# A four-layer graph attention kernel: rows between the layers kept unscaled, their roots taken once a layer

## The chip, the cores and the metric

The kernel runs on one core of a Trainium2 chip. The metric is device microseconds (us) of one execution, as a median over runs; lower is better. Engines are called PE (TensorE), DVE (VectorE), ACT (ScalarE), POOL (GpSimd) and SP (the queue that issues most DMAs).

## The reference, cut to what matters

```python
# N = 50000 nodes, E = 12500 edges sorted by target, D = 128
h = relu(layernorm(x)); x = x + conv(h)            # a graph convolution
h = relu(layernorm(x))
for l in range(4):                                 # _gat_layer
    h = x_l @ W[l]; e = ea @ We[l]
    alpha = leaky_relu((h @ a_s)[src] + (h @ a_d)[dst] + e @ a_e, 0.2)
    alpha = segment_softmax(alpha, dst)            # over the edges into one node, and a self loop
    out = segment_sum(h[src] * alpha, dst) + b
    x_l = (out - mean(out)) * rsqrt(var(out) + 1e-5) * g + beta
out = x + x_4
```

Every node has a self loop. A node without an incoming edge needs only its own row: that is the dense part. Nodes with edges, at most 12500 of them, go through the graph part.

## The kernel before, in words

Edges lie in 100 tiles (`C`) of 125 (`P`). `S` holds for each edge the row of its source node, `T` the row of its target node; one extra tile of `T` (index `C`) holds rows of segments that cross a border between tiles. A row has 130 numbers (`W`): the 128 features and two scores, which come out of the same matrix product, since the attention vectors are two more columns of the weights (`WCX`). The mean is taken out through centred weights, so the variance is the mean of the squares.

After setup and the convolution, the kernel runs four times:

1. **Dense stage** (`dense`, 16 groups of 500 nodes): all nodes through everything, with dense arithmetic. Beside it POOL issues 100 indirect gathers (`refresh`, L1535) that fetch into `S` the rows of the last layer from the DRAM table `row_t`.
2. **Score stage** (first block of `attention`, L1547 to L1615): the score columns are turned by PE transposes, then one long chain on DVE over arrays of 100x125 does the softmax. ACT takes the exponents; SP loads the masks `M` meanwhile.
3. **Loop** (second block of `attention`): 50 pairs of tiles. For pair n: DVE `mask` (L1779) and POOL `diagonal` (L1663) make the weights, PE `aggregate` (L1689, L1691) sums edges into target rows, ACT `copy_t` (L1739) copies them out of PSUM, PE `multiply_t` (L1710) multiplies by the weights, DVE `add_bias_t` (L1805) adds the bias into `T`. The source rows get the same product: PE `turn` (L200), DVE `copy_s` (L1801), PE `multiply_s` (L1710), DVE `add_bias_s` (L1811). Then ACT `squares` (L1749, L1754) and `root` (L1761), DVE `invert` (L1817), `rescale_t` (L1834) and `rescale_s` (L1841) normalise both. DVE `edge` (L1792) keeps two columns for the crossing rows. In layers 0 to 2 SP stores `T` to `row_t` in ten chunks (L1652). Layer 3 (`final`) has no source rows; POOL scatters the result to the output instead (L216).
4. **Crossing rows**: a short serial chain over one 100-row tile, L1722 to L1728 on PE, L1768 and L1771 on ACT, L1858 and L1866 on DVE, then a store (L1654).

The order on each engine is written by hand: `run_slot(t, NU, [(lag, op), ...])` issues in slot t the operation `op` for pair t - lag, in the order of the list. Engines meet through semaphores alone. Buffers and PSUM banks rotate over four pairs (`NS`); the T product and the aggregate of a pair share a bank, as do the turned S tile and the S product. A pair is in a slot of its own on every engine, and the slot's length in a steady run is the interval at which pairs complete.

All blocks end with a barrier over the engines.

## Time and profile before

| | |
|---|---|
| median of 3 runs | 2232.75 us (2230.29 to 2233.54) |
| profiled execution | 2236.65 us, of which the span is 2234.9 us |
| granted TensorE clock, mean over the span | 0.867 |
| busy in the span | PE 74%, weight loads 55%, DVE 78%, ACT 67%, POOL 52% |
| DMA | 145.21 MB, mean 65 GB/s |

Of the span, 1371 us are the four rounds of dense stage, score stage and loop; the rest is setup, the convolution and a longer dense stage. The busy shares are means over stages with different limits, so they don't say what limits a loop. In a timeline the start-to-start distance of two instructions of one engine tells what an instruction costs its engine; the duration shown also has its last part, which overlaps the next instruction. One fp32 matrix product stands in the trace as two MATMUL records.

### The profile page before, as it was taken

The numbers are of one execution on the slowest core, as the hardware profiler recorded it, in microseconds if no ns is written. First come the engines' busy times: TensorE is split into PE (matmuls) and PEld (weight loads), VectorE is DVE, ScalarE is ACT, GpSimd is POOL, SyncE is SP. The second block draws the span as 40 slices with busy tenths as digits, with TensorE's granted clock in tenths as the row PEclk, the third lists the DMA queues.
The fourth block names the chain that finished last, engine by engine and source line by source line (L and its number), as shares of the span: only waits on it lengthen the run. The fifth ranks groups of instructions, "written<-read, shape, count | busy, mean of one in ns | idle before, by whom it ended". The sixth has DMA issues, their size and how long they took to land. (4 is left out here: it accounts for less than half of the span.)

```text
span 2234.9 us, 41269 instructions
## 1 busy us (share of the span) xinstructions
PE 1663.9 (74%) x9595; PEld 1239.8 (55%) x9595; DVE 1751.1 (78%) x8774; ACT 1496.0 (67%) x7686; POOL 1154.6 (52%) x1069
## 2 busy tenths in 40 slices
PE   2589388888488885884996884996884996984980
PEld 1589255555277773552884552884552884542760
DVE  3680599999489995895996895996995996895870
ACT  0352299999389994992765992765992765992540
POOL 0477777400045555774225774225774225773777
PEclk9995599999689996996996996996996996995985
DMA  8013323321312123113113113113113113124321
GB/s 144 21 39 97 94 66 98 87 59 43 84 36 66 53 69 78 43 47 84 37 58 88 43 47 84 36 60 86 43 47 84 36 60 87 43 47 107 90 75 35
DMA packets 123138, 145.21 MB, mean 65 GB/s; under 512 B 56197, under 2 KB 83637, under 8 KB 122145
## 3 DMA queue, kind: packets, MB, share of 16 engines
q1 hardware_dynamic: 66303, 116.40, 19.1%
q0 software_dynamic: 56160, 25.40, 5.7%
q8 instruction: 78, 1.28, 0.3%
q14 instruction: 165, 1.35, 0.2%
q10 hardware_dynamic: 432, 0.79, 0.1%
HBM read 94.60 MB, written 67.86 MB: 73 GB/s over the span
## 5 line engine op out<-in xcount | busy, mean ns | idle before, releaser
L212 POOL DMA_INDIRECT S<-row_t,rowI x400 | 540.3, 1351 | 224.0 <-issue 224.0
L944 PE MATMUL bank<-AC,XT 128*125 128x390 f32 x800 | 330.5, 519 | 0.3
L1008 ACT ACTIVATE R<-bank 125x128 f32<-125x128 f32 x1200 | 323.2, 308 | 0.0
L1008 ACT ACTIVATION_READ_ACCUMULATOR R<-bank 125x1 f32 x1200 | 278.5, 242 | 0.0
L1663 POOL TENSOR_TENSOR R<-ident,aselfS 125x250 f32<-125x250 f32 x150 | 95.3, 637 | 333.7 <-PE bank L1691 257.8
L200 PEld LDWEIGHTS bank<-ident,Y 125*128 125x128 f32 x800 | 98.4, 150 | 215.3 <-issue 150.3
L200 PE MATMUL bank<-ident,Y 125*128 125x125 f32 x800 | 131.3, 290 | 115.2 <-ACT XT L992 52.0
L1710 PE MATMUL bank<-WCX,XT 128*125 128x130 f32 (+1 forms) x1400 | 210.2, 289 | 2.6 <-ACT XT L1739 2.4
L1739 ACT ACTIVATE XT<-bank 128x250 f32<-128x250 f32 x200 | 76.0, 380 | 190.6 <-PE bank L1691 182.4
L1689 PE MATMUL bank<-R,S 125*128 125x125 f32 x800 | 174.3, 300 | 33.9 <-DVE R L1779 27.6
L1050 DVE BATCH_NORM_STATS2 st<-R 125x6 f32<-125x128 f32 x800 | 173.0, 278 | 31.5 <-issue 31.1
L1710 PEld LDWEIGHTS bank<-WCX,XT 128*125 128x125 f32 x1400 | 184.1, 190 | 11.9 <-ACT XT L1739 4.9
L212 POOL DMA_INDIRECT S<-in_x,srcI x100 | 131.3, 1313 | 112.0 <-issue 112.0
L924 PEld LDWEIGHTS bank<-AC,XT 128*125 128x125 f32 x800 | 105.8, 204 | 117.4 <-ACT SB L1025 109.5
L924 PE MATMUL bank<-AC,XT 128*125 128x128 f32 x800 | 125.1, 303 | 58.5 <-ACT SB L1025 54.0
L216 POOL DMA_INDIRECT out_rows<-T,repNI x101 | 122.7, 1215 | 74.6 <-DVE T L1831 44.3
L944 PEld LDWEIGHTS bank<-AC,XT 128*125 128x125 f32 x800 | 134.4, 197 | 45.2 <-issue 10.4
L1689 PEld LDWEIGHTS bank<-R,S 125*128 125x128 f32 x800 | 124.6, 196 | 62.0 <-DVE R L1779 51.7
L1691 PE MATMUL bank<-R,T 125*128 125x125 f32 x800 | 158.8, 281 | 0.0
L212 POOL DMA_INDIRECT T<-in_x,dstI x101 | 136.1, 1348 | 40.6 <-issue 40.6
L1030 ACT ACTIVATE R<-bank 125x128 f32<-125x128 f32 x400 | 107.9, 313 | 39.9 <-PE bank L928 38.4
L207 PE MATMUL bank<-W,R 128*125 128x128 f32 x800 | 129.7, 311 | 0.0
(425 smaller groups left out, 5122.1 us busy)
## 6 DMA issues: line engine op xcount, KB each, us to landing
row_t<-T SPq DMA_DIRECT2D x40, 568.8 KB
R<-in_x SPq DMA_DIRECT2D x100, 224.0 KB
out_rows<-R SPq DMA_DIRECT2D x100, 224.0 KB
R<-m_t SPq DMA_DIRECT2D x5, 2734.4 KB
S<-row_t,rowI POOLq DMA_INDIRECT x400
T<-in_edge_attr SPq DMA_DIRECT2D x1, 5600.0 KB
x_t<-XB SPq DMA_DIRECT2D x50, 112.0 KB
R<-x_t SPq DMA_DIRECT2D x25, 224.0 KB
```

What stands on the lines that cost most here:

```text
L200: ins = nc.tensor.transpose(ps[:, a * P:(a + 1) * P], t, ident[0:P, 0:P])
L207: ins = nc.tensor.matmul(pz[0:P, a, :], xt[:, a * P:(a + 1) * P], w, start=False, stop=True, skip_group_check=True)
L212: pool.indirect_dma_start(to, None, table, bass.IndirectOffsetOnAxis(ap=idx, axis=0), bounds_check=rows - 1, oob_is_err=False).then_inc(do ...
L216: pool.indirect_dma_start(table, bass.IndirectOffsetOnAxis(ap=idx, axis=0), frm, None, bounds_check=rows - 1, oob_is_err=False).then_inc(d ...
L924: nc.tensor.matmul(last_of(g)[:, a, :], h0(g, a), AC[3], start=a == 0, stop=False, skip_group_check=True)
L944: nc.tensor.matmul(LAYERS[a][0:P, 0:3 * D + 6], h0(g, a), ACB[:, 0:3 * D + 6], start=True, stop=True).then_inc(layers_done.s, 1)
L1008: ins = nc.scalar.activation(JUNK[:, a * 3 + l, :], LAYERS[a][0:P, l * D:(l + 1) * D], ACT.Square, scale=D ** -0.5, accum_out=NRM[:, g % N ...
L1030: ins = nc.scalar.activation(JUNK[:, 12 + a, :], last_of(g)[:, a, :], ACT.Square, scale=D ** -0.5, accum_out=ss4[:, g % NS, a:a + 1])
L1050: ins = nc.vector.bn_stats(ring[:, a, :], v[:, a, :])
L1689: nc.tensor.matmul(o, S[:, 2 * n + a, 0:D], MA[:, r, a, :], start=True, stop=False, skip_group_check=True)
L1691: ins = nc.tensor.matmul(o, T[:, 2 * n + a, 0:D], DGB[:, r, a, :], start=False, stop=True, skip_group_check=True)
L1710: ins = nc.tensor.matmul(product(banks[bank + r], 2 * P)[:, a, :], XT[:, r, xt + a * P:xt + (a + 1) * P], WCX[:, l, 0:cols], start=not fin ...
```

## The change

Rows between layers 0, 1, 2 and 3 are kept unscaled. A row has 131 numbers (`RW`): the new column holds the mean of squares, which ACT's `squares` writes straight into it. `row_t` has rows of 131 numbers. In layers 0 to 2 `root`, `invert`, `rescale_t` and `rescale_s` are gone from the loop. At the head of the score stage of layers 1 to 3 ACT takes the roots of the whole column at once, DVE inverts them and scales the score columns before PE turns them; the inverse is multiplied into the edge weights (`alphaS`, `aselfS`, `DG`) and, for the source rows, into `add_bias_s`, which becomes two instructions for a pair instead of one. The order of every loop engine is rewritten: of layers 0 to 2 on PE, ACT and DVE, of the final layer on ACT. The crossing rows are copied unscaled, and their square stands in the same column.

```diff
+RW = W + 1
-        S = sb("S", [P, C, W])
-        T = sb("T", [P, TC, W])
+        S = sb("S", [P, C, RW])
+        T = sb("T", [P, TC, RW])
-        row_t = nc.dram_tensor("row_t", [P * TC, W], F32, kind="Internal").ap()
+        row_t = nc.dram_tensor("row_t", [P * TC, RW], F32, kind="Internal").ap()
...
+                    if l:
+                        dve.wait_ge(*rooted.at(1))
+                        ch.add(nc.vector.reciprocal(sx[:, 1:2], sx[:, 0:1]))
+                        ch.link(nc.vector.reciprocal(rrT[:, :], rrT[:, :]))
+                        nc.vector.tensor_scalar(sx[:, 3:5], T[0:C, C, D:W], sx[:, 1:2], None, ALU.mult)
+                        nc.vector.tensor_tensor(scT[:, :, :], T[:, 0:C, D:W],
+                                                rrT[:, :].unsqueeze(2).broadcast_to([P, C, 2]),
+                                                ALU.mult).then_inc(scored.s, 1)
+                        dve.wait_ge(*rooted.at(2))
+                        ch.link(nc.vector.reciprocal(rrS[:, :], rrS[:, :]))
+                        nc.vector.tensor_tensor(scS[:, :], S[:, :, D], rrS[:, :], ALU.mult).then_inc(scored.s, 1)
                     dve.wait_ge(*columns_in.at(1))
...
+                    if l:
+                        nc.vector.tensor_tensor(alphaS[:, :], banks[0][0:P, 0:C], rrS[:, :], ALU.mult)
+                        nc.vector.tensor_tensor(aselfS[:, :], banks[0][0:P, C:2 * C], rrT[:, :], ALU.mult)
+                        nc.vector.tensor_scalar(DG[:, :], ident[0:C, 0:C], car1[:, 1:2], sx[:, 1:2], ALU.mult, ALU.mult)
...
+                    if l:
+                        nc.scalar.activation(rrT[:, :], T[:, 0:C, W], ACT.Sqrt, bias=epsc[:, 0:1])
+                        nc.scalar.activation(sx[:, 0:1], T[0:C, C, W:RW], ACT.Sqrt,
+                                             bias=epsc[0:C, 0:1]).then_inc(rooted.s, 1)
+                        nc.scalar.activation(rrS[:, :], S[:, :, W], ACT.Sqrt, bias=epsc[:, 0:1]).then_inc(rooted.s, 1)
                     act.wait_ge(*act_in.at(1))
...
-                        run_slot(t, NU, [(0, aggregate), (1, multiply_t)] if final else [(4, multiply_s), (4, multiply_t), (3, aggregate), (0, turn)])
+                        run_slot(t, NU, [(0, aggregate), (1, multiply_t)] if final else [(3, multiply_t), (0, turn), (2, multiply_s), (1, aggregate)])
...
+                            ins = nc.scalar.activation(Y[:, r, a, :], T[:, 2 * n + a, 0:D], ACT.Square, scale=D ** -0.5,
+                                                       accum_out=T[:, 2 * n + a, W:RW])
+                        ins.then_inc(t_ready.s, 1)
...
-                        run_slot(t, NU, [(4, squares), (2, copy_t), (4, root)])
+                        run_slot(t, NU, [(3, root), (1, copy_t), (2, squares)] if final else [(2, squares), (0, copy_t)])
...
-                        nc.vector.tensor_tensor(S[:, 2 * n:2 * n + 2, :], product(banks[4 + n % NS], 2 * P),
-                                                BB[:, l:l + 1, :].broadcast_to([P, 2, W]), ALU.add).then_inc(bias_s.s, 1)
+                        for a in range(2):
+                            z = product(banks[4 + n % NS], 2 * P)[:, a, :]
+                            if l:
+                                ins = nc.vector.scalar_tensor_tensor(S[:, 2 * n + a, 0:W], z, rrS[:, 2 * n + a:2 * n + a + 1],
+                                                                     BB[:, l, :], ALU.mult, ALU.add)
+                            else:
+                                ins = nc.vector.tensor_tensor(S[:, 2 * n + a, 0:W], z, BB[:, l, :], ALU.add)
...
-                        run_slot(t, NU, [(0, diagonal), (0, mask), (4, rescale_t), (3, invert), (1, edge)] if final else [(0, mask), (1, add_bias_s), (0, copy_s), (1, add_bias_t), (2, edge), (3, invert), (5, rescale_t), (3, rescale_s)])
+                        run_slot(t, NU, [(0, diagonal), (0, mask), (4, rescale_t), (3, invert), (1, edge)] if final else [(0, mask), (2, add_bias_t), (1, add_bias_s), (0, copy_s), (4, edge)])
...
+                    if not final:
+                        dve.wait_ge(*x_pe.at(3))
+                        stage(nc.vector.tensor_copy(T[0:C, C, 0:W], banks[2][0:C, 0:W]), 3)
+                        return
```

The order of DVE in one slot of the loop of layer 1, before; `bank4` to `bank7` hold products of source rows, `bank0` to `bank3` those of target rows, `rr4` is the inverse root:

```order
L1779 TENSOR_TENSOR R<-R,alphaS 125x250
L1811 TENSOR_TENSOR S<-bank4,BB 125x260
L1801 COPY XT<-bank5 128x250
L1805 TENSOR_TENSOR T<-bank0,BB 125x260
L1792 COPY EDGE<-XT 128x4
L1817 RECIPROCAL rr4<-rt4 125x4
L1834 TENSOR_TENSOR T<-T,rr4 125x260
L1841 TENSOR_TENSOR S<-S,rr4 125x260
```

And in the changed kernel, with lines of its own file:

```order
L1824 TENSOR_TENSOR R<-R,alphaS 125x250
L1850 TENSOR_TENSOR T<-bank1,BB 125x2x130
L1859 SCALAR_TENSOR_TENSOR S<-bank6,rrS,BB 125x130 x2
L1846 COPY XT<-bank7 128x250
L1837 COPY EDGE<-XT 128x4
```

Three instructions of a slot are gone, one became two, and the T bias now stands ahead of the S bias and belongs to the pair before it.

PE in one slot of the same loop, before:

```order
L1710 MATMUL bank5<-WCX,XT 125x130 x2
L1710 MATMUL bank1<-WCX,XT 125x130 x2
L1689 MATMUL bank2<-R,S 128x125
L1691 MATMUL bank2<-R,T 128x125
L1689 MATMUL bank2<-R,S 128x125
L1691 MATMUL bank2<-R,T 128x125
L200 MATMUL bank5<-ident,S 128x125 x2
```

And changed (L1748 is the product, L205 the transposes, L1727 and L1729 the aggregate):

```order
L1748 MATMUL bank1<-WCX,XT 125x130 x2
L205 MATMUL bank4<-ident,S 128x125 x2
L1748 MATMUL bank6<-WCX,XT 125x130 x2
L1727 MATMUL bank3<-R,S 128x125
L1729 MATMUL bank3<-R,T 128x125
L1727 MATMUL bank3<-R,S 128x125
L1729 MATMUL bank3<-R,T 128x125
```

The ten products and transposes are the same; the two products now stand apart with the transposes between them, and the T product runs one aggregate later than the S product.

DVE at the head of the score stage of layer 1 in the changed kernel; before, the stage begins with the multiplication of `bank2`:

```order
L1568 RECIPROCAL sx<-sx 100x1
L1569 RECIPROCAL rrT<-rrT 125x100
L1570 TENSOR_SCALAR sx<-T,sx 100x2
L1571 TENSOR_TENSOR scT<-T,rrT 125x200
L1575 RECIPROCAL rrS<-rrS 125x100
L1576 TENSOR_TENSOR scS<-S,rrS 125x100
L1564 TENSOR_TENSOR tmp<-bank2,repN 100x125
```

Six instructions stand ahead of what was the first one, and PE's three transposes wait for them.

## Rows read from the trace of the kernel before

**Rows 1.** Stages: dense, loop of layer 1, final loop; busy us per engine, PE clock.
```profile
1192.50:1370.00 177.50, 134.27 (x576) 79.53 (x576) 142.04 (x832) 139.69 (x800) 134.91 (x100) 0.85 0.24 57
...
1391.00:1527.00 136.00, 119.89 (x908) 109.79 (x906) 126.49 (x404) 88.61 (x504) 31.34 (x50) 0.96 0.16 49
...
2060.40:2235.00 174.60, 105.27 (x658) 87.40 (x658) 92.14 (x355) 60.47 (x304) 122.73 (x101) 0.77 0.28 71
```

**Rows 2.** Groups by form, layer 0's loop: count, busy us, mean ns, idle before.
```profile
L1841 DVE TENSOR_TENSOR S<-S,rr 125x260 f32<-125x260 f32 x42 | 33.3, 793 | 0.0
...
L1663 POOL TENSOR_TENSOR R<-ident,aselfS 125x250 f32<-125x250 f32 x39 | 24.9, 637 | 74.4 <-PE bank L1691 74.4
...
L1834 DVE TENSOR_TENSOR T<-T,rr 125x260 f32<-125x260 f32 x42 | 16.4, 391 | 0.0
```

**Rows 3.** Timeline, a steady slot of layer 0: start us, duration us.
```profile
1110.32 0.41 DVE L1779 TENSOR_TENSOR R<-R,alphaS 125x250 f32<-125x250 bf16 x1
...
1112.02 0.64 POOL L1663 TENSOR_TENSOR R<-ident,aselfS 125x250 f32<-125x250 f32 x1 [1.91 <-PE bank L1691]
1112.12 0.82 DVE L1841 TENSOR_TENSOR S<-S,rr 125x260 f32<-125x260 f32 x1
...
1112.87 0.41 DVE L1779 TENSOR_TENSOR R<-R,alphaS 125x250 f32<-125x250 bf16 x1
...
1113.20 0.41 DVE L1811 TENSOR_TENSOR S<-bank,BB 125x260 f32<-125x260 f32 x1
...
1113.33 0.49 PE L1689 MATMUL bank<-R,S 125*128 125x125 f32 x2 [0.21 <-DVE R L1779]
```

**Rows 4.** Timeline, first slots of layer 1's loop.
```profile
1396.53 1.13 PE L1710 MATMUL bank<-WCX,XT 128*125 128x130 f32 x8
...
1397.24 0.43 DVE L1811 TENSOR_TENSOR S<-bank,BB 125x260 f32<-125x260 f32 x1 [0.67 <-PE bank L1710]
...
1398.60 1.13 PE L1710 MATMUL bank<-WCX,XT 128*125 128x130 f32 x8
...
1399.56 0.38 PE L1689 MATMUL bank<-R,S 125*128 125x125 f32 x2
...
1403.74 0.60 POOL L1663 TENSOR_TENSOR R<-ident,aselfS 125x250 f32<-125x250 f32 x1 [2.44 <-PE bank L1691]
1403.77 0.84 DVE L1779 TENSOR_TENSOR R<-R,alphaS 125x250 f32<-125x250 bf16 x1
```

**Rows 5.** Timeline, two DVE instructions on PSUM, final loop.
```profile
2074.62 0.60 DVE L1824 SCALAR_TENSOR_TENSOR T<-bank,rr,G 125x128 f32<-125x128 f32 x2
```

**Rows 6.** Timeline, end of layer 1's loop and its crossing rows.
```profile
1516.15 0.39 PE L1691 MATMUL bank<-R,T 125*128 125x125 f32 x2
...
1521.82 0.43 PE L1722 MATMUL bank<-ident,EDGE 128*100 128x128 f32 x1 [4.10 <-DVE T L1834]
...
1525.69 0.29 ACT L1771 ACTIVATE sx<-sx,epsc 100x1 f32<-100x1 f32 x1
...
1526.66 0.28 SPq L1654 DMA_DIRECT2D row_t<-T  x1
```

**Rows 7.** Timeline, score stage of layer 1.
```profile
1370.68 0.43 PE L1596 MATMUL bank<-ident,S 125*100 125x125 f32 x1 [8.34 <-PEq L872]
...
1371.57 0.29 DVE L1555 TENSOR_TENSOR tmp<-bank,repN 100x125 f32<-100x125 f32 x1 [3.72 <-PE bank L1598]
...
1386.98 0.94 DVE L1583 RECIPROCAL mx<-mx 100x125 f32<-100x125 f32 x1
```

**Rows 8.** Stages again, inside that score stage (last numbers: DMA share, GB/s).
```profile
1384.00:1386.00 2.00, 0.13 (x1) 0.13 (x2) 1.64 (x6) 0.00 (x0) 0.00 (x0) 0.50 0.00 0
```

**Rows 9.** Timeline, head of the final loop.
```profile
2068.44 1.28 ACT L1761 ACT_TABLE_LOAD   x1
...
2072.92 1.23 POOL L216 DMA_INDIRECT out_rows<-T,repNI  x1 [38.98 <-DVE T L1831]
```

**Rows 10.** Timeline, first ACT instruction of the dense stage of layer 1.
```profile
1198.15 0.30 ACT L974 ACTIVATE rt<-mv,epsc 125x4 f32<-125x4 f32 x1 [6.76 <-DVE mv L1057]
```

133 lines of the change are left out of this document (69 added, 64 removed).

## The prediction, made before the changed kernel was timed

> **What bounds the kernel now.** I read the table of stages first [rows 1]. Layer 1's round is a dense stage of 177.5 us, a score stage of some 21 us and a loop with its crossing rows of 136 us; layers 0 and 2 are like it. The change leaves the dense arithmetic alone, so three loops of 136 us are where time can come from. In a loop DVE is busy for 126.5 us of the 136, PE for 119.9, ACT for 88.6, POOL for 31. Busy times overlap, so next comes the timeline of one steady slot [rows 3]: `mask` starts at 1110.32 and again at 1112.87, 2.55 us later, and between them DVE has no gap. PE, on the other hand, starts its aggregate only after a wait for that `mask`. So DVE sets the pace.
>
> One of its instructions stands out: `rescale_s` takes 793 ns in the mean, `rescale_t` of the same shape 391 [rows 2]. POOL's `diagonal` runs from 1112.02 to 1112.66 [rows 3]; `rescale_s` starts at 1112.12 and ends at 1112.94, just 0.28 us behind POOL's end. At 1403.77 it is `mask` that starts 0.03 us behind POOL and then takes 0.84 us instead of 0.41 [rows 4]. So a DVE instruction with both inputs in SBUF that begins while POOL's works is held until POOL is done. The Trainium skill says the same (SBUF — State Buffer, section Who interferes with whom): the second input of such an instruction comes through a read interface that GpSimd also uses, whoever starts first keeps it, and an instruction with at most one SBUF input is not touched. By that rule, with which the trace agrees in those two rows, the hold isn't removed with `rescale_s`; it looks for `mask`, the only such instruction left in the slot. That is my first rival.
>
> What is next below DVE? In the first slots of layer 1's loop, before `rescale_s` is in play, PE's products start at 1396.53 and 1398.60 [rows 4]: 2.07 us a slot, with no idle time of PE noted. That is PE's own pace for its ten products and transposes at the full clock.
>
> **The loop of layers 0 to 2.** DVE, start to start: 2.55 us, less 0.75 for `rescale_s` (1112.12 to 1112.87, the hold in it), less 0.31 for `rescale_t` (0.391 less the 0.08 by which instructions overlap, as in `mask`, 0.41 long and 0.33 to the next one [rows 3]), leaves 1.49; `invert` goes too, worth under 0.1, left in as reserve. `add_bias_s` cost 0.33 and becomes two. Two such instructions on PSUM, 128 columns each, take 0.60 us [rows 5], so 0.52 to the next: plus 0.19, 1.68 in all. In layer 0 the two are plain additions, between 0.33 and 0.52; DVE has then 1.5 to 1.7. The Trainium skill (VectorE: DVE Perf Modes, section The TRN2 errata) gives a fixed 120 cycles of 0.96 GHz to each instruction that reads PSUM; by that estimate the split would cost 0.125 and not 0.19. A held `mask` adds 0.43: 2.1 us.
> ACT: 88.6 us for 50 pairs is at most 1.77 us a slot [rows 1], and `root` goes. POOL: one `diagonal` of 0.64. PE: the same ten, 2.07. So PE becomes the bound, with DVE close by. Are PE's inputs there in time? With the lags of the lists, and DVE working in the same time as PE's next slot, `aggregate` and `multiply_s` take what DVE made a slot before, `multiply_t` what ACT made two slots before. The tightest round is: `multiply_s` starts, 0.71 us later DVE can start on its result (1396.53 to 1397.24) [rows 4], then 0.52 for the two bias instructions, 0.33 for `copy_s`, and the next `multiply_s` about 0.1 later: 1.66, under 2.07. For `mask` it is 0.71 + 0.52 + 0.33 + 0.07 + 0.41, some 2.04 from the start of `multiply_s`; the aggregate that needs it starts a slot and one product after that, 2.07 + 0.45. Half a microsecond of slack without the hold, none with it. I take 2.07 for layer 0 and 2.10 for layers 1 and 2.
> Some five slots at the head already run at PE's pace, and PE starts at the half clock there in both kernels. So 45 slots count: 45 x 0.48 = 21.6 us in layer 0, 45 x 0.45 = 20.2 in layers 1 and 2.
>
> **The end of the loop.** Before, the last aggregate stands at 1516.15 and the first crossing product at 1521.82, 5.67 us later, after a wait for `rescale_t` [rows 6]. Lags of four and five slots become two and three; `root`, `invert` and `rescale_t` are off the way. Left: copy 0.4, product 0.7, bias 0.4, squares of a pair and a half at under 1.77 a pair, some 1.8. That is 3.3: a gain of 2.3, between 0.5 and 3. In the crossing rows the root (0.29 at 1525.69) and its inverse leave the way to the store at 1526.66, and the square now waits for a copy instead of PSUM: a gain of 0.4. Together 2.7 a layer.
> Loops: 24.3 + 22.9 + 22.9 = 70.1 us.
>
> **The score stage of layers 1 to 3** now starts later. Before, PE's first transpose is at 1370.68 and DVE's first instruction at 1371.57 [rows 7]. Now: two roots on ACT, 0.29 each and overlapping, 0.5; the inverse of 100 columns, for which the row of 125 columns has 0.94, so 0.78 by columns; two scalings, 0.35; the second inverse 0.78; one scaling 0.2; then the last transpose as before. That is 2.6, less 0.1 since the two T transposes no longer stand ahead: 2.5 us. Nothing hides it: DVE's chain is serial, and the load of the masks, which SP waits for in this stage, is long over by 1384, where DMA moves nothing [rows 8], so it isn't what ends the stage either. Bounds: 2.0, if inverses overlap more, and 3.5, if each link costs another 0.2. Times three: 7.5 us lost.
>
> **Head and tail of others.** The final loop ends with POOL's scatters: 101 from 2072.92 to the end, 1.6 us apiece [rows 1, 9]. It gains what its first one gains. That waits for a root, ahead of which stands a table load of 1.28 us at 2068.44, and ACT's copy stood between squares and root; now the root follows the squares directly. Gain 1.0, between 0 and 1.5. In layers 0 to 2 the table load leaves the loop for the dense stage's first root, before which ACT idles 6.76 us [rows 10]: nothing. Rows of 131 numbers instead of 130: 0.8% more bytes in a gather, and POOL is busy 134.9 of 177.5 us there [rows 1]; nothing, at worst 1 us a stage. The memsets at the start lie beside the first loads.
>
> **Sum**: 70.1 - 7.5 + 1.0 = 63.6 us off 2236.65 of the profiled execution, which is 2173. The median shown is 3.9 lower than that execution, which would make 2169. I say 2171. With slots of 2.07 to 2.15 and the bounds above, its own range is 2163 to 2181.
>
> **Rivals.**
> A. The hold moves to `mask` and PE waits for it in every slot. For it: the row at 1403.77. POOL starts when an aggregate has ended, as it did beside `rescale_s`; from its start to the end of the held `mask` it is 0.87 us [rows 4], and I take 0.35 between PE's last aggregate record and POOL's start, since the 0.71 above is three records at 0.12 and such a rest; 0.05 comes behind the mask. PE's other work between two aggregates is its products, 0.96 (1398.60 to 1399.56) [rows 4], and of the remaining 1.11 some 0.2 for transposes, the aggregate's 0.9 apart; so the hold exceeds it by 0.1, and an aggregate after a wait starts slower by another 0.1. Slot 2.25. Against it: once PE is late, `mask`, released by another product, comes ahead of POOL and isn't held, so it should dither. Price: 45 x (0.18 + 0.15 + 0.15) = 21.6, time 2193.
> B. PE, now almost without gaps, is granted less clock. The loop has 0.96 and the dense stage 0.85 [rows 1]; at the latter a slot would be 2.07 x 0.96 / 0.85 = 2.34, loops gain 135 x 0.21 + 8.1, so 36.5, and the time is 2201. Against it: the low means hold the restarts after barriers.
> C. Slower: the new order makes PE and DVE wait for each other in turn. If the mask of a slot were needed by the aggregate of the same slot, the round would be `multiply_s` to held mask, 0.71 + 0.52 + 0.33 + 0.07 + 0.75 + 0.05 = 2.43, and the aggregate's 0.9: 3.3 us, and the time 2171 + 135 x 1.2 = 2333. It decides from a slot of 2.56 us on, since 8.1 and 1.0 gained and 7.5 lost nearly cancel. Against it: the lags put a slot between producer and consumer.
> D. The loops gain nothing, since something else than DVE paces them at 2.5. Then 2231. Against it: the 2.07 of [rows 4].
>
> **Chances.** My forecast 0.70, A 0.17, B 0.06, C 0.03, D 0.02, others on the slow side 0.02. A measurement of this kernel can tell about 0.2%, 4.5 us. Forecast, A and B are all faster: faster 0.94, within 0.2% 0.02, slower 0.04. The range takes in A: 2160 to 2193.
>
> **What would show it.** Right: in the three loops aggregates start every 2.07 to 2.15 us, PE has no idle time noted, DVE idles before its biases, waiting for products; loop stages of 112 to 114 us; score stages of layers 1 to 3 longer by 2.5 with two reciprocals of some 0.8 at the head; POOL's first scatter 11 to 12 us after the loop's start. `mask` at 0.41 in the mean speaks for me, at 0.8 with PE waiting for it for A; a clock under 0.95 in the loop for B. I am wrong if a loop stage is above 120 us.

## The result, and the profile after

| | before | changed |
|---|---|---|
| median of four runs, us | 2232.85 (2230.29 to 2233.54) | 2156.47 (2152.42 to 2159.09) |
| ratio, 95% interval | 1 | 0.9658 [0.9639, 0.9678] |
| profiled execution, span, us | 2234.9 | 2157.3 |

The change takes 76.4 us off, 3.4%. I had forecast 2171, with a range down to 2160: right in direction and in what bounds the loops before and after, too small in size. The time is 3.5 us below the range, and the largest single miss, the dense stages, is of a mechanism that the forecast left out.

The same stages as in [rows 1], of the changed kernel: the dense stage, the loop of layer 1 and the final loop. The columns are those of the rows before: stretch, its length, busy us of PE, PEld, DVE, ACT, POOL, the granted clock, DMA share, GB/s.
```profile
1165.00:1340.00 175.00, 131.80 (x576) 77.87 (x576) 142.88 (x834) 141.70 (x805) 134.33 (x100) 0.86 0.24 59
...
1361.00:1475.00 114.00, 108.35 (x908) 105.01 (x908) 94.63 (x305) 80.43 (x452) 34.03 (x50) 0.96 0.19 60
1984.00:2157.00 173.00, 100.09 (x658) 83.97 (x658) 92.05 (x356) 64.64 (x304) 122.31 (x101) 0.79 0.28 72
```
DVE's busy time in the loop fell from 126.5 to 94.6 us. PE is now busy for 108 of the loop's 111.5 us: it is the bound, as forecast. In layers 1 and 2 a hold of `mask` adds to it, as shown below.

Where the time went, by stage, in the two profiled executions. A loop is counted from its first `mask` to the store of the crossing rows; a dense stage from the start of its first statistics to the start of its last sum; "to scores" is from there to the first operation on the scores. All lengths are taken between starts in the traces, before rounding.

| us | before | changed | gain | forecast |
|---|---|---|---|---|
| first to last `mask`, layers 0, 1, 2 | 124.4, 124.3, 124.2 | 98.9, 103.6, 103.6 | 66.9 | 62.0 |
| last `mask` to store, layers 0 to 2 | 11.7, 11.7, 11.7 | 8.0, 8.0, 8.0 | 11.3 | 8.1 |
| dense, layers 1 to 3 | 170.3, 170.0, 171.0 | 167.8, 167.6, 167.6 | 8.4 | 0 |
| to scores, layers 1 to 3 | 4.4, 4.4, 4.4 | 7.2, 7.4, 9.2 | -10.6 | -7.5 |
| final loop to the end | 174.1 | 172.6 | 1.5 | 1.0 |
| sum | | | 77.5 | 63.6 |

The spans differ by 77.6 us, so the table misses nothing of size. It shows four misses that matter: the slots, the ends of the loops, the dense stages, and the way to the scores.

**The slots.** Two neighbouring slots of layer 1's loop in the changed kernel, from its timeline (start us, duration us, engine, line, operation):
```profile
1402.66 0.61 POOL L1701 TENSOR_TENSOR R<-ident,aselfS 125x250 f32<-125x250 f32 x1 [1.25 <-PE bank L1729]
1402.72 0.83 DVE L1824 TENSOR_TENSOR R<-R,alphaS 125x250 f32<-125x250 bf16 x1
...
1403.60 0.49 PE L1727 MATMUL bank<-R,S 125*128 125x125 f32 x2
...
1404.72 0.41 DVE L1824 TENSOR_TENSOR R<-R,alphaS 125x250 f32<-125x250 bf16 x1
1404.84 0.75 POOL L1701 TENSOR_TENSOR R<-ident,aselfS 125x250 f32<-125x250 f32 x1 [1.57 <-PE bank L1729]
...
1405.70 0.38 PE L1727 MATMUL bank<-R,S 125*128 125x125 f32 x2
```
At 1402.72 `mask` (L1824) starts 0.06 us behind POOL and takes 0.83; the aggregate that needs it starts at 1403.60 and at 0.49 is slower than in the next slot, where it takes 0.38. In that next slot `mask` comes first, takes 0.41, and it is POOL that takes longer, 0.75 instead of 0.61. The forecast's rival A and the argument against it are both true here, every second time. From `mask` to `mask`, 2.17 or 2.18 us and 2.00 alternate, 2.09 in the mean. In layer 0, where the two bias additions are plain ones, `mask` is always first, and PE's products are exactly 2.00 us apart:
```profile
1091.42 0.61 PE L1748 MATMUL bank<-WCX,XT 128*125 128x130 f32 x4
1091.86 0.38 PE L1727 MATMUL bank<-R,S 125*128 125x125 f32 x2
...
1093.41 0.61 PE L1748 MATMUL bank<-WCX,XT 128*125 128x130 f32 x4
...
1095.41 0.61 PE L1748 MATMUL bank<-WCX,XT 128*125 128x130 f32 x4
```
So PE's own pace is 2.00, not the 2.07 that I read from [rows 4]. (One MATMUL row merges neighbouring records, here four; the 2.00 is from start to start.)

**The crossing rows.** The end of layer 1's loop, changed kernel, which answers to [rows 6]:
```profile
1466.46 0.39 PE L1729 MATMUL bank<-R,T 125*128 125x125 f32 x2
...
1469.80 0.33 PE L1760 MATMUL bank<-ident,EDGE 128*100 128x128 f32 x1 [1.50 <-ACT Y L1790]
...
1470.52 0.47 PE L1762 MATMUL bank<-MF,END 100*128 100x100 f32 x2 [0.39 <-DVE END L1892]
...
1471.80 0.47 PE L1766 MATMUL bank<-WCX,XTX 128*100 128x130 f32 x2
...
1473.12 0.27 SPq L1692 DMA_DIRECT2D row_t<-T  x1
```
The same products in the kernel before, which [rows 6] left out:
```profile
1522.64 0.75 PE L1724 MATMUL bank<-MF,END 100*128 100x100 f32 x2 [0.38 <-DVE END L1853]
...
1524.50 0.76 PE L1728 MATMUL bank<-WCX,XTX 128*100 128x130 f32 x2
```
From the last aggregate to the first crossing product it is 3.34 us instead of 5.67: the forecast's 3.3. From there to the store it is 3.32 instead of 4.84, where I had put a gain of 0.4. Each product got shorter too: before, PE had stood idle for 4.10 us and ran at half the clock; now it has been idle for 1.50 and still runs at the full one. The granted clock, the third number from the end, falls at 1521.4 in the kernel before, ahead of the first crossing product and 5.3 us before the store:
```profile
1516.40:1521.40 5.00, 1.29 (x10) 0.90 (x8) 4.41 (x18) 3.49 (x20) 0.00 (x0) 1.00 0.41 130
1521.40:1526.40 5.00, 2.64 (x8) 1.66 (x8) 1.10 (x5) 0.66 (x3) 0.00 (x0) 0.50 0.41 130
```
In the changed kernel it falls at 1472.8, behind the last crossing product and 0.3 us before the store:
```profile
1467.80:1472.80 5.00, 2.17 (x12) 1.36 (x11) 2.09 (x10) 2.54 (x17) 0.00 (x0) 1.00 0.41 130
1472.80:1477.80 5.00, 0.00 (x0) 0.00 (x0) 0.00 (x0) 1.58 (x3) 1.54 (x2) 0.50 0.37 102
```

**The score stage** of layer 1, changed kernel, answering to [rows 7]:
```profile
1339.64 0.76 DVE L1569 RECIPROCAL rrT<-rrT 125x100 f32<-125x100 f32 x1
...
1340.86 0.77 DVE L1575 RECIPROCAL rrS<-rrS 125x100 f32<-125x100 f32 x1
...
1342.53 0.29 DVE L1564 TENSOR_TENSOR tmp<-bank,repN 100x125 f32<-100x125 f32 x1 [0.54 <-PE bank L1629]
```
The two inverses take 0.76 and 0.77, forecast 0.78; the whole takes 2.8 to 3.0 us a layer instead of 2.5. Layer 3 lost 2.0 more, because POOL's last gather there ended at 1957.1, 0.4 us behind the end of the dense stage's last sum:
```profile
1955.86 1.27 POOL L217 DMA_INDIRECT S<-row_t,rowI  x1 [0.30 <-issue]
...
1962.22 0.45 ACT L1643 ACTIVATE rrS<-S,epsc 125x100 f32<-125x100 f32 x1
```

**The dense stage.** Its arithmetic is the same in both kernels. Stretches of ten us at its head, layer 2, where the kernel before has its first statistics at 1531.9:
```profile
1532.00:1542.00 10.00, 4.78 (x17) 3.36 (x17) 6.88 (x43) 3.56 (x9) 7.98 (x7) 0.50 1.05 245
1542.00:1552.00 10.00, 8.14 (x25) 5.14 (x25) 8.39 (x52) 6.61 (x27) 8.13 (x6) 0.50 0.13 25
1552.00:1562.00 10.00, 8.82 (x37) 5.89 (x37) 6.20 (x40) 8.44 (x43) 8.18 (x6) 0.82 0.09 13
```
And the changed kernel, first statistics at 1477.9:
```profile
1478.00:1488.00 10.00, 4.77 (x17) 3.36 (x17) 6.87 (x43) 3.55 (x9) 8.17 (x7) 0.50 1.01 255
1488.00:1498.00 10.00, 8.14 (x30) 5.48 (x30) 8.51 (x52) 6.74 (x27) 8.17 (x7) 0.57 0.13 24
1498.00:1508.00 10.00, 7.88 (x31) 4.95 (x30) 6.28 (x41) 8.62 (x43) 8.17 (x7) 0.78 0.08 13
```
The clock is half in both at first (0.50). In the changed kernel it comes back 18.8 us after the first statistics, within the second ten us (0.57), in the kernel before after 23.6 us, in the third.

### The profile page after: what moved, and what is told of

It is laid out like the page before. It is cut to its first block and busy times, and to the rows that moved or that the text cites. A ratio compares the mean times of both kernels' runs of the same rounds, so it can differ in the third digit from the quotient of the medians.

```text
span 2157.3 us, 40845 instructions
## 1 busy us (share of the span) xinstructions
PE 1612.2 (75%) x9595; PEld 1213.7 (56%) x9595; DVE 1652.0 (77%) x8491; ACT 1482.4 (69%) x7542; POOL 1167.8 (54%) x1069
## 5 line engine op out<-in xcount | busy, mean ns | idle before, releaser
L1015 ACT ACTIVATION_READ_ACCUMULATOR R<-bank 125x1 f32 x1200 | 271.5, 231 | 0.0
L1701 POOL TENSOR_TENSOR R<-ident,aselfS 125x250 f32<-125x250 f32 x150 | 107.5, 719 | 261.1 <-PE bank L1729 182.9
L1748 PE MATMUL bank<-WCX,XT 128*125 128x130 f32 (+1 forms) x1400 | 218.9, 280 | 0.0
L205 PEld LDWEIGHTS bank<-ident,Y 125*128 125x128 f32 x800 | 98.8, 150 | 210.3 <-issue 159.9
L205 PE MATMUL bank<-ident,Y 125*128 125x125 f32 x800 | 131.5, 290 | 110.8 <-ACT XT L999 46.7
L1748 PEld LDWEIGHTS bank<-WCX,XT 128*125 128x125 f32 x1400 | 182.9, 189 | 6.3 <-issue 0.4
L1727 PE MATMUL bank<-R,S 125*128 125x125 f32 x800 | 164.9, 288 | 10.1 <-DVE T L1881 6.6
L1729 PE MATMUL bank<-R,T 125*128 125x125 f32 x800 | 158.4, 280 | 0.0
L1727 PEld LDWEIGHTS bank<-R,S 125*128 125x128 f32 x800 | 125.2, 197 | 18.1 <-issue 10.7
L1037 ACT ACTIVATE R<-bank 125x128 f32<-125x128 f32 x400 | 107.3, 310 | 38.8 <-PE bank L935 37.5
L1790 ACT ACTIVATE Y<-T 125x128 f32<-125x128 f32 x300 | 90.2, 301 | 60.4 <-DVE T L1850 60.4
```

Of the source, the lines that this page charges most:

```text
L205: ins = nc.tensor.transpose(ps[:, a * P:(a + 1) * P], t, ident[0:P, 0:P])
L1015: ins = nc.scalar.activation(JUNK[:, a * 3 + l, :], LAYERS[a][0:P, l * D:(l + 1) * D], ACT.Square, scale=D ** -0.5, accum_out=NRM[:, g % N ...
L1701: nc.gpsimd.tensor_tensor(DGB[:, n % NS, :, :], ident[0:P, 0:P].unsqueeze(1).broadcast_to([P, 2, P]), aselfS[:, 2 * n:2 * n + 2].unsqueeze ...
L1727: nc.tensor.matmul(o, S[:, 2 * n + a, 0:D], MA[:, r, a, :], start=True, stop=False, skip_group_check=True)
L1729: ins = nc.tensor.matmul(o, T[:, 2 * n + a, 0:D], DGB[:, r, a, :], start=False, stop=True, skip_group_check=True)
L1748: ins = nc.tensor.matmul(product(banks[bank + r], 2 * P)[:, a, :], XT[:, r, xt + a * P:xt + (a + 1) * P], WCX[:, l, 0:cols], start=not fin ...
```

## The experiments

All stage lengths below come from one profiled execution of each kernel. Up to layer 0's loop all kernels do the same work, but for two memsets, the width of a row and, in two of them (e11 and e12), transposes in layer 0's score stage. Yet that loop starts anywhere between 1050.1 and 1056.0 us (1057.8 in e11); so the stages tell more than the totals. The ratios are each to the kernel before in the same session. Compare the kernels by them: a difference of a few us between two medians of different sessions is not clear of noise where the intervals overlap.

| kernel | median, us | ratio to before | loops 0, 1, 2 | dense 1, 2, 3 |
|---|---|---|---|---|
| before | | | 136.2, 136.1, 135.9 | 170.3, 170.0, 171.0 |
| changed | 2156.47 | 0.9658 [0.9639, 0.9678] | 106.9, 111.5, 111.6 | 167.8, 167.6, 167.6 |
| e2_new_order | 2226.53 | 0.9964 [0.9952, 0.9977] | 135.3, 135.1, 135.1 | 168.0, 170.4, 170.9 |
| e3_old_order | 2159.20 | 0.9665 [0.9647, 0.9683] | 111.1, 111.3, 111.6 | 167.9, 167.6, 169.0 |
| e4_pool_behind_mask | 2149.57 | 0.9629 [0.9609, 0.9648] | 107.4, 107.4, 107.7 | 169.1, 167.6, 167.1 |
| e7_busy_pe | 2232.02 | 0.9990 [0.9970, 1.0010] | 134.8, 136.5, 136.2 | 169.9, 170.2, 170.9 |
| e7b_busier_pe | 2225.66 | 0.9969 [0.9957, 0.9981] | 135.1, 135.1, 135.5 | 167.8, 170.0, 168.4 |
| e1_wide_rows | 2231.92 | 1.0012 [0.9989, 1.0035] | 136.2, 136.1, 136.0 | 170.4, 170.4, 170.2 |
| e1b_shift | 2231.74 | 1.0001 [0.9991, 1.0011] | 136.1, 136.1, 135.9 | 170.3, 170.1, 170.9 |
| e10_before_warm_dense | 2226.69 | 0.9977 [0.9966, 0.9989] | 136.3, 136.7, 136.6 | 166.7, 169.8, 166.6 |
| e9_warm_dense | 2158.05 | 0.9666 [0.9650, 0.9683] | 107.8, 111.3, 111.3 | 169.3, 168.6, 167.7 |
| e11_warm_loop | 2157.72 | 0.9660 [0.9642, 0.9679] | 107.2, 110.4, 111.2 | 167.4, 169.9, 167.7 |
| e6_final_old | 2158.45 | 0.9661 [0.9622, 0.9700] | 107.0, 111.4, 111.8 | 167.7, 167.2, 168.8 |
| e8_hide_roots | 2153.49 | 0.9641 [0.9621, 0.9661] | 107.0, 111.3, 110.9 | 170.1, 168.2, 170.3 |
| e12_together | 2144.88 | 0.9611 [0.9593, 0.9629] | 107.4, 107.4, 107.3 | 167.0, 167.2, 167.2 |
| e13_masks_roots | 2143.53 | 0.9585 [0.9546, 0.9625] | 107.2, 107.0, 107.6 | 167.9, 169.9, 166.8 |

### Order or work?

The kernel before with the changed order:
```diff
-[(4, multiply_s), (4, multiply_t), (3, aggregate), (0, turn)]
+[(3, multiply_t), (0, turn), (2, multiply_s), (1, aggregate)]
-[(4, squares), (2, copy_t), (4, root)]
+[(3, root), (2, squares), (0, copy_t)]
-[(0, mask), (1, add_bias_s), (0, copy_s), (1, add_bias_t), (2, edge), (3, invert), (5, rescale_t), (3, rescale_s)]
+[(0, mask), (2, add_bias_t), (1, add_bias_s), (0, copy_s), (4, edge), (3, invert), (4, rescale_t), (4, rescale_s)]
```


> The kernel before, with all its arithmetic (rescale_t, rescale_s, root and invert in the loops), but its slots of layers 0 to 2 in the changed order: PE [(3, multiply_t), (0, turn), (2, multiply_s), (1, aggregate)], ACT [(3, root), (2, squares), (0, copy_t)], DVE [(0, mask), (2, add_bias_t), (1, add_bias_s), (0, copy_s), (4, edge), (3, invert), (4, rescale_t), (4, rescale_s)]. My theory (the work taken off DVE is what counts): DVE stays the bound with its slot of 2.5 us, the loops change by the shorter tail alone, at most 2 us each; time 2226 to 2235. Rival (the order is what counts, since in the old one each engine waits for results of the same slot): a slot near 2.1 us and a time under 2180.

Measured 2226.53. The slots stay at 2.54 us, as before, and the loops are 0.9 to 1.0 shorter. DVE's work bounds them in either order; the order alone is worth about 1 us a loop. That comes from the first slots and not, as I had thought, from a shorter tail: from the last `mask` to the store it is 12.0 us here, 11.7 before.

The changed kernel with the old order, that is with the lags of the kernel before on PE, on DVE for the operations that are left, and on ACT `[(4, squares), (2, copy_t)]`:

> The changed kernel with its new arithmetic, but the old lags in layers 0 to 2: PE [(4, multiply_s), (4, multiply_t), (3, aggregate), (0, turn)], ACT [(4, squares), (2, copy_t)], DVE [(0, mask), (1, add_bias_s), (0, copy_s), (1, add_bias_t), (2, edge)]. The 2.07 us that I took for PE's own pace is 2.00 in the changed kernel. Theory 1: the 0.07 was PE's wait for ACT's copy of the same slot, which the old lags put between aggregate and multiply_t; then this kernel has slots of 2.07 or more, and its longer tail costs 1 to 2 us a layer: 45 x 0.07 + 1.5 = 4.6 a layer in layer 0 and up to that in layers 1 and 2, time 2162 to 2175. Theory 2: it was the SBUF traffic of rescale_s and rescale_t that slowed PE; then the slot of layer 0 stays 2.00 and only the tail is paid, 2158 to 2162. Rival: the order is necessary, and the time goes above 2200.

Measured 2159.20, a ratio of 0.9665 against the 0.9658 of the changed kernel: the same within noise. The order of layers 0 to 2 is not what the change gains by. Its tail, from the last `mask` to the store, is 8.2 to 8.3 us, so the new arithmetic alone gives 3.5 of the 3.7 us by which the tail got shorter. The time is just below theory 1's range and inside theory 2's; the slot decides between them. Its timeline, layer 0:
```profile
1091.60 0.38 ACT L1777 ACTIVATE XT<-bank 128x250 f32<-128x250 f32 x1 [0.53 <-PE bank L1729]
1091.62 1.13 PE L1748 MATMUL bank<-WCX,XT 128*125 128x130 f32 x8
...
1092.58 0.38 PE L1727 MATMUL bank<-R,S 125*128 125x125 f32 x2
...
1093.67 0.38 ACT L1777 ACTIVATE XT<-bank 128x250 f32<-128x250 f32 x1 [0.53 <-PE bank L1729]
1093.69 1.13 PE L1748 MATMUL bank<-WCX,XT 128*125 128x130 f32 x8
```
The slot is 2.07 us with no `rescale_s` anywhere, so SBUF traffic (theory 2) is out. ACT's copy, which `multiply_t` needs, starts together with the products: `multiply_s` covers most of it, and the remainder is a wait that the view doesn't note. It shows in the starts: from the eight product rows to the next aggregate it is 0.96 us here (1091.62 to 1092.58), as in [rows 4] (1398.60 to 1399.56), while in the changed kernel four of them take 0.44 (1091.42 to 1091.86), so eight 0.88. That is the 0.07 in the 2.07 that I took. In layers 1 and 2 this kernel loses nothing against the changed one: its slower round starts `mask` 0.13 us ahead of POOL every time, so its slots are 2.07 without a hold instead of 2.09 with one.

### The hold of `mask`

```diff
                         if n >= NS:
                             pool.wait_ge(*gathered.at(n - NS + 1))
+                            pool.wait_ge(*masked.at(n - NS + 2))
                         nc.gpsimd.tensor_tensor(DGB[:, n % NS, :, :], ...
```


> The changed kernel; POOL's diagonal of slot n in layers 0 to 2 (and 3) also waits for the mask of slot n-2 (the last one issued, which has by then ended or is about to), so that POOL never starts just ahead of a mask. Theory: in layers 1 and 2 every second mask is held by POOL (0.83 instead of 0.41 us), which makes slots of 2.00 and 2.18 in turn; with POOL behind the mask all slots are 2.00, a gain of 45 x 0.09 = 4 us in each of the layers 1 and 2, none in layer 0: 2156.5 - 8 = 2148. Rival 1: the alternation comes from DVE's two scalar_tensor_tensor, 0.61 instead of 0.49, and not from the hold: slots unchanged, 2156. Rival 2: the diagonal now comes late for its aggregate and PE waits for POOL: slots of 2.1 or more in all layers, 2160 to 2170.

(The mask waited for is that of slot n-3, one earlier than this says. DVE's list runs that far behind POOL's, and it is the latest one.) Measured 2149.57, a ratio of 0.9629, which is 6.5 us less than the changed kernel's 0.9658 gives. The loops are 107.4 to 107.7 in all layers, in sum 7.5 us less than in the changed kernel. A slot of layer 1:
```profile
1399.85 0.41 DVE L1825 TENSOR_TENSOR R<-R,alphaS 125x250 f32<-125x250 bf16 x1
...
1400.41 0.60 POOL L1702 TENSOR_TENSOR R<-ident,aselfS 125x250 f32<-125x250 f32 x1 [1.39 <-DVE R L1825]
```
POOL starts 0.15 us after the mask's end, neither holds the other, and slots are 2.00. In layers 1 and 2 the hold cost 4 us each; it is removed by a wait on an engine with time to spare, and not by less work. The Trainium skill (SBUF — State Buffer, section Who interferes with whom) says that a DVE instruction with two SBUF inputs contends with a GpSimd instruction that reads SBUF, and that the order of issue decides who is blocked. Both orders of the pair above agree: the later one is longer, whichever it is (0.83 for 0.41 us, 0.75 for 0.61).

### The clock in the crossing rows

The kernel before with 14 (below: 30) additional transposes ahead of its crossing rows:
```diff
+                    if not final:
+                        for k in range(14):
+                            nc.tensor.transpose(banks[4][0:P, 0:P], ident[0:P, 0:P], ident[0:P, 0:P])
                     pe.wait_ge(*edged.at(NU))
```


> The kernel before, with 14 additional transposes (of the identity into a bank that nothing reads any more) between PE's last product and the crossing rows of layers 0 to 2, where PE is idle for 4.1 us. In before the crossing chain's PE instructions take 0.43, 0.75, 0.76 us, in the changed kernel 0.33, 0.47, 0.47 after an idle time of 1.5 us. Theory: that is the granted clock, which the idle time costs; here the same chain takes 0.33, 0.47, 0.47 with all of before's arithmetic, and the time from the first crossing product to the store falls from 4.85 to 3.9 us, 3 us in all: 2230. Rival: the crossing chain's gain comes from the root and the inverse that went, and the clock has no part: the durations stay as in before, 2233, or a little more if the additional transposes delay the chain.

Inconclusive at first: PE's idle time fell only to 2.58 us. In layer 0 the crossing products took 0.47 and the loop became 1.4 us shorter; those of layers 1 and 2 stayed as before.

> The kernel before with 30 additional transposes between PE's last product and the crossing rows of layers 0 to 2. With 14 of them (1.69 us) the idle time went from 4.10 to 2.58 us; layer 0's crossing chain then took 0.33, 0.47, 0.47 and those of layers 1 and 2 still 0.43, 0.75, 0.76. With 30 (3.6 us) the idle time is some 0.7 us. Theory (the granted clock falls with idle time): all three chains at 0.33, 0.47, 0.47, each 1.0 us shorter from the first crossing product to the store; the three loops sum to some 405 us instead of 408.2. Rival (chance, or a property of layer 0): layers 1 and 2 stay at 0.43, 0.75, 0.76.

Idle time 0.83 us, layer 1:
```profile
1512.05 3.44 PE L1722 MATMUL bank<-ident 125*125 125x125 f32 x30
1516.33 0.33 PE L1725 MATMUL bank<-ident,EDGE 128*100 128x128 f32 x1 [0.83 <-DVE T L1837]
1517.04 0.47 PE L1727 MATMUL bank<-MF,END 100*128 100x100 f32 x2 [0.38 <-DVE END L1856]
...
1518.33 0.47 PE L1731 MATMUL bank<-WCX,XTX 128*100 128x130 f32 x2
```
All three chains take 0.33, 0.47 and 0.47 us a product, as at the full clock, and the loops sum to 405.7 us, with root and inverse still in them. From the first crossing product to the store it is 3.9 us, where the kernel before takes 4.84 and the changed one 3.32. So of the 1.5 us that the changed kernel gains here a layer, 1.0 is the clock, which it keeps when PE is idle for 1.50 us instead of 4.10; 0.5 is the rest, the root and the inverse, forecast at 0.4. One number I had not expected: two of the three dense stages that follow also took 168 us.

### The dense stage: rows, addresses or the clock

Only the wider rows, their last column a constant, all work as before:
```diff
+RW = W + 1
-        S = sb("S", [P, C, W])
-        T = sb("T", [P, TC, W])
+        S = sb("S", [P, C, RW])
+        T = sb("T", [P, TC, RW])
```


> The kernel before with rows of 131 numbers in S, T and row_t instead of 130, the last one a constant that nothing reads; all work as before. From a layer's first statistics to its last sum the dense stages of layers 1 to 3 took 170.4, 170.1 and 171.0 us before, 511.5 in all, and 503.1, 504.4, 503.8 in the three kernels with the new arithmetic, a gain of 7 to 8 us that I had not forecast. Theory W (the wider rows, their stride in SBUF or in the gathers, or the addresses that they shift): here too 503 to 505 with the old arithmetic, time 2225. Rival N (something that the loops leave behind, such as ACT's table, loaded now at the dense stage's head): 510 to 512 here, time 2233. Rows of 0.8% more bytes were forecast to cost at most 1 us a stage: 514 would show that.

Only the addresses, by `GAP = sb("GAP", [D, 201])` ahead of `R`:

> The kernel before with an unused tensor of 201 numbers a partition in front of the buffer R, so that all buffers behind it lie at the addresses that they have in the changed kernel; rows stay 130 wide. If the dense stage's gain comes from addresses alone: dense stages of layers 1 to 3 sum to 503 to 505 us, 2225. If from the width of the rows or from what the loops leave behind: 510 to 512, 2233.

Neither: sums of 511.0 and 511.2 us for 511.4 before, and times within 0.2% of before. The wider rows cost nothing either, as forecast.

Then the clock. PE is given work in the 6 us at the head of the dense stages of layers 1 to 3, once in the kernel before and once in the changed one:
```diff
+                    if first_group > SHARES[0]:
+                        for k in range(24):
+                            nc.tensor.transpose(banks[3][0:P, 0:P], ident[0:P, 0:P], ident[0:P, 0:P])
                     for t in slots:
                         run(t, [(5, last_layer), ...
```


> The kernel before with the same 24 transposes at the head of the dense stages of layers 1 to 3; all else as before, with the root and inverse work in the loops. If the dense stage's gain is the clock's and nothing else of the change, the sum of the three dense stages falls from 511.5 to 505 or below, and the time to 2226 or below. If it is something that the loops leave behind in the changed kernel (ACT's table, the rows' last column), it stays 509 to 512.

Sum 503.1 us, within 0.2 us that of the changed kernel (502.9), without anything of the change. Head of layer 1's dense stage (first statistics at 1192.2; it took 166.7 us):
```profile
1192.00:1202.00 10.00, 5.11 (x31) 3.85 (x30) 7.89 (x51) 4.12 (x10) 8.17 (x7) 0.84 1.03 247
1202.00:1212.00 10.00, 8.82 (x33) 6.08 (x33) 7.45 (x44) 7.14 (x28) 8.17 (x7) 0.62 0.17 34
```
and of layer 2's (1526.2; 169.8 us):
```profile
1526.00:1536.00 10.00, 5.90 (x29) 4.68 (x28) 6.86 (x42) 3.31 (x8) 8.17 (x7) 0.67 1.05 242
1536.00:1546.00 10.00, 8.26 (x25) 4.88 (x23) 8.61 (x54) 6.54 (x25) 8.17 (x7) 0.50 0.23 41
```
The stage in which the clock was half through the second ten us is the long one. The same holds over the 48 dense stages of all runs here: the 25 with a granted clock of 0.53 or more in the second ten us take 166.5 to 169.1 us; of the 23 with 0.50, twenty take 169.8 to 171.0, and two of the other three (167.9, 168.2 and 169.3) have more clock than any other stage but one in the twenty us after that, 0.88.

Layer 0's dense stage is a control that no kernel was built for: it has none of the change's new work and none of the transposes, in any kernel. There too the clock comes back 18.6 to 19.8 us after the first statistics in 11 kernels, and the stage takes 167.8 to 169.4 us; in the other five it comes back after 23.3 to 24.9 us, and the stage takes 169.8 to 170.4.

Which of the two returns a stage gets goes with the time from the clock's fall, at the end of the loop before, to the stage's first statistics. For the 39 stages of layers 1 to 3 that have no transposes at their head:

| fall to first statistics, us | first statistics to return, us | stages |
|---|---|---|
| 4.6 to 5.7 | 18.2 to 19.3 | 17 |
| 5.8 to 7.1 | 23.6 to 25.0 | 8 |
| 9.1 | 18.2 | 1 |
| 9.3 to 10.6 | 23.6 to 24.8 | 13 |

The three stages of the kernel before are in the last group, those of the changed kernel in the first, since its clock falls 5 us later against the store. So the clock returns early in 14 of the 15 stages of the kernels with the new arithmetic and an unchanged dense head (the changed one, e3, e4, e6, e11), and in 1 of 12 with the old (before, e1, e1b, e2). That it is the fall and not the arithmetic is borne out by e7b, which has the old arithmetic and moves the fall by its 30 transposes alone: its stages have 5.7, 6.0 and 5.3 us, and the return is early, late and early, as the table has it. The groups were read from the traces afterwards. Why they lie where they do is not shown, and layer 0's stages, whose clock falls 21 to 25 us ahead of the statistics, are not covered by them.

In e10 not all of the gain arrives: the intervals from store to next loop sum to 593.1 instead of 596.7, since the score stage waits for POOL's 100 gathers, which do not get shorter.

> The changed kernel with 24 additional transposes (of the identity, into a bank that nothing reads) on PE at the head of the dense stages of layers 1 to 3, where PE is idle for the 6 us before its first rows. Rows 131 wide alone and shifted addresses alone left before's dense stages at 510.9 and 511.3 us in sum, so the 8 us don't come from these. By the windows of the trace PE's granted clock, half since the crossing rows, returns to full 18 us after the first statistics in the changed kernel, and 23 us after them in before; of the 24 dense stages read so far nearly all in which it returns within 20 us take 167.1 to 169.1 us, all others but one 169.9 to 171.0. Theory (the time at which the clock returns): with PE busy from the stage's start it returns sooner still, at 10 to 14 us, and a stage takes 165 to 167; sum 498 to 500 instead of 503.1, time 2152. Rival (the clock returns when it does, whatever PE does in the idle 6 us): sum 503, 2156. Rival 2: the transposes delay the first turn: sum 504 or more.

A miss: 2158.05, sum 505.6. The transposes raise the clock early (0.67 in the first ten us of layer 2), but it falls again in the pauses that follow, and in this kernel it came back within 20 us in all three stages anyway. Here layer 1's came back for good only after 23.0 us.

> The changed kernel with 9 additional transposes on PE in the score stage, in the 2.4 us between the last carry and the weights, and 4 behind the transposes of the weights; in all four layers. PE's clock is half for the first 5.3 us of a loop (to 1366.95 in layer 1) and full after that. Theory (activity before the loop brings the clock back sooner): full 2 to 3 us sooner, and since PE is the bound there each loop is 1 to 1.5 us shorter: 105.6, 110.2, 110.3 and the time 2151. Rival: the score stage's chain is held up by the transposes, op to mask 19.1 becomes 19.5 or more, and nothing is gained: 2156 to 2158.

A miss as well, 2157.72. In layer 1 the clock is full 2.4 us after the loop's start instead of 5.4 and the loop is 1.1 us shorter; but in layers 0, 2 and 3 it was full after 4.4, 4.8 and 6.3 us, against 3.8, 5.5 and 3.5 in the changed kernel. When it comes back varies by 4 us, and the work that I gave PE did not decide it. Nor was the clock lost in the pause before a loop alone: it had been half since 44 to 51 us before it came back, from the last part of the dense stage on.

### The final loop

The changed kernel with `[(4, squares), (2, copy_t), (4, root)]` on ACT in the final loop:

> The changed kernel with the final loop's old ACT order [(4, squares), (2, copy_t), (4, root)] instead of [(3, root), (1, copy_t), (2, squares)]. POOL's first scatter came 12.4 us after the final loop's start before and 10.5 after. Theory: the order alone moves it; here 12.4 again, and all scatters follow: 1.9 us longer from the loop's start to the end (174.5), 2158. Rival (the table load moved off, or another part of the change, did it): 10.5 and 2156.5.

POOL's first scatter comes 11.2 us after the loop's start, and 173.7 us are left from that start to the end. Before it was 12.1 and 174.1, in the changed kernel 10.2 and 172.6 (I had written 12.4 and 10.5, each too high by 0.3). The rows of the changed kernel that answer to [rows 9], with the table load still in the chain:
```profile
1990.23 1.28 ACT L1801 ACT_TABLE_LOAD   x1
...
1994.92 1.23 POOL L221 DMA_INDIRECT out_rows<-T,repNI  x1 [37.79 <-DVE T L1881]
```
The difference of 1.0 us between this kernel and the changed one is not the order's alone, since the clock came back at different times in the two. All kernels here have one of the two orders in the final loop, so they can be set side by side where the clock came back alike (us after the loop's start):

| clock full, old order | first scatter | clock full, new order | first scatter |
|---|---|---|---|
| 3.4 (e1b) | 10.6 | 3.5 (changed) | 10.2 |
| 4.0 (e7b) | 10.9 | 4.0 (e12) | 10.4 |
| 4.8 (e6) | 11.2 | 5.0 (e9) | 10.8 |
| 6.7 (before) | 12.1 | 6.6 (e13) | 11.2 |

At an equal clock the order is worth 0.4 us, and 0.9 where the clock comes late. Of the 1.9 us between before and changed the rest, 1.0 to 1.5, goes with the clock, which was full after 3.5 us in one and 6.7 in the other. From the first scatter to the end the kernels take 161.6 to 163.5 us, without regard to the order. The totals, 2158.45 and 2156.47, cannot tell any of this apart.

### Better versions

The roots, inverses and scalings of T's columns go to the head of the dense stage, where DVE waits 5 us for its first rows, and the inverse for S behind the first scan of the scores:
```diff
+                    if ahead:                                   # dense stage, ACT
+                        nc.scalar.activation(rrT[:, :], T[:, 0:C, W], ACT.Sqrt, bias=epsc[:, 0:1])
...
+                        nc.vector.reciprocal(rrT[:, :], rrT[:, :]).then_inc(t_inverted.s, 1)   # DVE
...
+                    if l:                                       # score stage, DVE
+                        seg.between = scale_source
                     seg.spread_masked(run[:, :], tmp[:, :])
```


> The changed kernel with the score stage's new work moved where engines wait. The roots, inverses and scalings of T's columns of layers 1 to 3 are made at the head of the dense stage, where DVE waits 5 us for its first rows (ACT's table load of 1.28 us stands there too); the inverse and scaling of S's column stand behind the first scan of the score stage, where DVE waits 0.5 us for PE's carry, and the S transpose behind that carry. From the dense stage's last sum to the first operation of the scores it is 4.4 us before and 7.2 in the changed kernel. Theory: the T chain (roots, two inverses, scalings) vanishes and the S chain costs 0.77 + 0.33 less 0.5: 4.5 us to the first operation, 0.6 us more from there to the first mask (19.7 instead of 19.1), 2.1 us gained a layer, 6.4 in all, 2150. Rival (the head of the dense stage isn't free, since its first root waits for ACT): the dense stages grow by the 1.3 us of this chain each and the gain halves: 2153. Rival 2: DVE's inverse beside PE's carry delays all that follows by its whole 1.1 us: 2152.

Measured 2153.49. To the scores it is 4.2 us instead of 7.2 and from there to the first mask 0.5 more, so 2.5 a layer was gained there, 7.5 in all. The dense stages gave back 5.7 (508.6 for 502.9), more than either rival had: their first statistics come 0.5 us later after the store, which puts all three into the group of 5.8 to 7.1 us above, and the clock came back in the second ten us in none of them.

> The changed kernel with POOL's diagonal behind the mask (slots of 2.00 in layers 1 and 2, 4 us each), the T roots at the dense stage's head and the S inverse behind the first scan (2.5 us a layer from the last sum to the first mask), the 24 transposes at the head of the dense stages of layers 1 to 3 and the 13 in the score stages. If the gains add up: 2156.5 - 7.5 (masks) - 7.5 (roots) - 4 (dense) - 4 (loops) = 2133. If the transposes do nothing and the roots at the head delay the dense stage as they did alone (sum 508.5 instead of 503.1): 2147.

> The changed kernel with POOL's diagonal behind the mask and with the roots, inverses and scalings moved, but without any additional transposes: what is left of the combination that ran at 2144.88. If the transposes have no worth there (a dense stage of the changed kernel gets its clock back within 20 us without them): 2142 to 2147, the three dense stages 503 to 505 and the intervals from store to loop 196.5 to 197.5. If they are what gave 167.0, 167.2 and 167.2 in that kernel, since the roots at the head delay the stage's first rows by 0.5 us and the clock then returned late in two stages of three (170.1, 168.1, 170.3): dense sum 507 to 510, time 2148 to 2152.

2144.88 with the transposes, 2143.53 without: the same, with overlapping intervals. The one without them is the best version, 12.9 us below the changed kernel's median. In the two traces the dense stages sum to 504.6 without transposes and to 501.3 with them, and from store to loop it is 594.1 and 590.1, since without them the clock came back late in two stages of three. I had expected it early there, and 196.5 to 197.5 us from store to loop; it was 197.0, 198.9 and 198.2. The medians show no gain from that, so the transposes are not worth keeping.

## Why the prediction fell short

- **Right**: DVE's pace before (2.54), `rescale_s` in the hold, PE as the next bound, the 3.3 us from the last aggregate to the first crossing product, the wider rows at nothing. No run tests the moved table load alone; the dense heads that now hold it show no loss. The two bias instructions take 0.61 us where I had 0.60 (1401.80 in layer 1, the next DVE instruction 0.53 later); as plain additions in layer 0 0.49. The split cost 0.07 us for the plain ones (0.49 less 0.42) and 0.19 for these. The estimate of 0.125 from the fixed cost that the Trainium skill gives (VectorE: DVE Perf Modes, section The TRN2 errata) lies between the two.
- **The term 45 x 0.48** (layer 0, 21.6 for a measured 25.5): it used 2.07 as "PE's own pace for its ten products". That number held a wait of 0.07 for ACT's copy, which the new order removes. The pace is 2.00, shown by layer 0 and, with the wait back, by the kernel with the old order. 45 x 0.07 are 3.2 of the 3.9 us. The count of 45 was off as well: only 40 slots ran at 2.54 before, and the first six intervals, which I had left as they were, got 3.2 us shorter (16.2 to 13.0). These two largely cancel, which is luck.
- **The terms 45 x 0.45** (layers 1 and 2) came out at 20.8 and 20.6 for 20.2 each. They are close only because two errors cancel: a pace that was too slow by 0.07, and a hold for which I had 0.03 us a slot where it was 0.09 in the mean. The hold is rival A's, with the 0.18 that A gave it, but in every second slot only. Rival B's price does not follow from its own terms (33.6 us less gain than the forecast makes 2205, not 2201); its clock did not occur, since the loop still has 0.96.
- **"In the crossing rows ... a gain of 0.4"**: 1.5. The clock, which went with the idle time ahead of the chain, was left out: 3 us in three layers.
- **"Gain 1.0" in the final loop**: 1.5, and near by luck. I had it from the order on ACT, which is worth 0.4 us at an equal clock; the rest is the clock's earlier return.
- **"The change leaves the dense arithmetic alone, so three loops ... are where time can come from"**: this is the step that failed most. Same arithmetic isn't same time: 8.4 us came from there, 2.0 of which the gathers took back. The kernel before with 24 transposes at that head shows that the clock's return does this without the change. What the traces show in its place: with the shorter tail the clock falls 5 us later, and the time from its fall to the stage's first statistics, with which an early or a late return went in all 39 stages, comes into the group of early ones. Why the groups lie where they do stays open.
- **The score stage**, 2.5: 2.8 to 3.0, and 2.0 more in layer 3 for the gathers, which I had not counted. The roots of T end 0.7 us after the stage's start (1338.88 to the first inverse at 1339.56), where I had 0.5.

The misses of size, 4.9 (slots), 3.2 (ends) and 5.3 (dense and scores together), and 0.5 at the end, are the 13.9 us between 63.6 and 77.5. All but the score stage's have one sign, and the range had allowed 11 us on that side. The loops alone would have left the time inside the range; what put it outside is the dense stages, in which I had seen nothing to gain.

## What to carry to other kernels

A pace read where another engine was not yet the limit can still hold a short wait that no idle time shows: compare the starts of one engine's rows with those of the same work elsewhere (0.96 us for eight products against 0.44 for four). When a change shortens a stretch in which PE idles, price the clock behind it too, in stages that the change does not touch. And when two engines exclude each other, look which starts first: making the one with spare time wait for the other gave 7 us for one line. And before a small difference is put down to an edit, check that the clock came back at the same time in both kernels: in the final loop it was worth more than the edit.
